# Moving the re-layout of a mode tensor from its load to its store: four mixing layers in one launch

## The chip, the cores and the metric

The program runs on one NeuronCore of a Trainium2 chip, in one launch. The metric is the time on the device in microseconds (us), from start to end of the program. The median of three runs of the kernel before is 8131.88 us (8118.62 to 8132.38).

## The reference, cut to what matters

The input is `x`, 16 images of 224 x 224 pixels with 32 channels, float32. Four layers follow each other, each of the form `x = x + layer(groupnorm(x))`. Only the last one is touched by the change:

```python
def _L3_conv_ref(x, R_real, R_imag):
    R = R_real + 1j * R_imag                       # (32, 32, 64, 64)
    kX, kY = R.shape[-2:]
    xt = jnp.moveaxis(x, -1, -3)
    xd = jsp_fft.dct(xt, type=2, axis=-1, norm='ortho')
    xf = jnp.fft.rfft(xd, axis=-2, norm='ortho')
    xtr = xf[..., :kX, :kY]                        # 64 x 64 modes are kept
    y = jnp.einsum('ijab,ejab->eiab', R, xtr)      # mix the channels, per mode
    yp = jnp.pad(y, ((0, 0), (0, 0), (0, nXf - kX), (0, nY - kY)))
    yr = jnp.fft.irfft(yp, n=nX, axis=-2, norm='ortho')
    yd = jsp_fft.idct(yr, type=2, axis=-1, norm='ortho')
    return jnp.moveaxis(yd, -3, -1)
...
x = x + _L3_conv_ref(_gn(x), L3_conv_R_real, L3_conv_R_imag)
```

So: for each of 16 images, 64 x 64 modes of 32 channels, each a complex number, are mixed over the channels by a matrix of their own, and are then taken back to pixels.

## The kernel before, in words

`program` (L1627) runs six passes one after the other, with nothing of one overlapping the next: `pass_fractal` (names a_), `mix_modes` for layer 1 (b1_), `pass_spectral` (c_), `pass_conv` (d_, which also makes the modes of layer 3 in `spec3`), `mix_modes` for layer 3 (b3_; the trace prints both calls as b_), and `pass_inverse` (e_). The last two are the ones touched.

**Mixing, third layer** (`mix_modes` with `groups=2`). The 64 x 64 modes of an image are folded into 2048 pairs: pair m = a' x 64 + b holds the modes (a', b) and (a' + 32, b), the fold being the index h of 0 and 1. The pairs are walked in 16 blocks of SC = 128. For a block SyncE (SP) loads 4 MB of matrices (`Rb`, L708, 32 KB per partition) and 1 MB of modes (`Xb`, L710, runs of 512 B) on its own DMA queue (q1). Both have two buffers, `par` 0 and 1. VectorE (DVE) negates a part of `Rb` (L744), scales `Xb` into the block diagonal `XB` (L746), both in two halves, and corrects one column (L750). TensorE (PE) makes 256 small matmuls (L783) into four PSUM banks. ScalarE (ACT) copies two of the banks into `Yb` (L799) and DVE the other two (L757). ACT then issues the stores to `y3` (L806) on its own DMA queue (q10): for each of 4 slot groups j and 2 folds h one DMA of 16 partitions (the 16 images) by 8 KB, 32 pairs of 64 floats, in one run on both sides. The next load into a buffer is issued when PE has done with it (`sp.wait_ge(mixed, ...)`). A `Yb` buffer is used again when its stores have landed: the waits on `out_[par]` stand before L757 on DVE and before L799 on ACT, each counting 16 x 8 = 128 for a block. PE waits for `low` and `high`, the two copies out of PSUM, of the block two before.

The 64 floats v of a pair are k x 32 + (re or im, channel half), where k is the half of the channels (even or odd channels).

**Inverse** (`pass_inverse`). For each of the 16 images SP loads, on q1, four mode pieces (L1448, one for each fold h and channel half k) and eight pieces of the residual `x3` (L1442, 784 KB each, runs of 1792 B) that is added at the end. A mode piece goes to 64 partitions (b) by 32 (a') by 32 floats:

```python
sp.dma_start(UT[64 * k:64 * k + 64, par, :, h, :],
             d["y3"][e, h].rearrange("(a b) v -> b a v", b=64)[:, :, 32 * k:32 * k + 32])
```

In `y3` and in `UT` the runs of this copy are 32 floats, 128 B. `UT` has two buffers, `X3` one, in four groups of 8 channels (lg). The modes and the residual of image e + 1 are issued as the groups of image e come free (`f_done`), the modes first. For each of 16 channel pairs cp, PE makes four matmuls over the columns (L1477: modes as weights, `UT`, two products of 224 columns, each in two passes), ACT copies the result to `V` (L1513), PE makes two products over the rows with the table `G3` (L1486; one row of the trace for each pass), and DVE adds the residual into `OUT` (L1532, four instructions). When 16 channel pairs are done GpSimd (POOL) issues eight stores of 784 KB to `out` (L1549) on its queue q0. PE runs at most two channel pairs ahead of DVE (`after(pe, sem["f_done"], e16 + (cp - 1))`).

`tables` (L1555) makes the constants on the host, among them `G3`, whose rows are in the order of the 128 rows of `V`: (a', fold h, re or im).

Of the kernel before, what the change touches and what calls it, by code (L numbers as in the profile page):

```python
# [27 lines left out]
C = 32  # L28
G = 16
T = 2  # L30
P = 128
# [46 lines left out]
def after(engine, sem, count):  # L78

    if not isinstance(count, int) or count > 0:  # L80
        engine.wait_ge(sem, count)  # L81
# [599 lines left out]
def mix_modes(nc, name, B, pairs, d, spec, out, R, acol, bcol, groups=1):  # L681
# [9 lines left out]
    nb = min(spec.shape[-1], SC)  # L691
    parts = SC // nb
    with Scope(nc, name) as z:
        Rb = z.sb("R", [P, 2, SC, 64])
# [35 lines left out]
        def _(dve):  # L730
# [22 lines left out]
            def collect(i, par):  # L753

                after(dve, out_[par], i * 128)
                dve.wait_ge(mixed, i * 4 + (2 * par + 2))
                dve.tensor_copy(Yb[:, par, SLOTS // 2:].rearrange("p s v -> p (s v)"),  # L757
                                PS[:, 4 * par + 2:4 * par + 4, :].rearrange("p k v -> p (k v)")).then_inc(high, 1)
# [34 lines left out]
        @block.scalar  # L793
        def _(act):
            def turn(i):
                for par in range(2):
                    after(act, out_[par], i * 128)
                    act.wait_ge(mixed, i * 4 + (2 * par + 1))
                    act.activation(Yb[:, par, 0:SLOTS // 2].rearrange("p s v -> p (s v)"),  # L799
                                   PS[:, 4 * par:4 * par + 2, :].rearrange("p k v -> p (k v)"), ACT.Copy)\  # L800
                       .then_inc(low, 1)
                    act.wait_ge(low, i * 2 + (par + 1))
                    act.wait_ge(high, i * 2 + (par + 1))
                    for j in range(4):
                        for h in range(2):
                            act.dma_start(out[:, h, bass.ds((i * 2 + par) * SC + SLOTS * j, SLOTS), :],  # L806
                                          Yb[32 * j + 16 * h:32 * j + 16 * h + B, par]).then_inc(out_[par], 16)

            turn(0)
            with act.Fori(1, n // 2) as i:  # L810
                turn(i)
            for par in range(2):
                act.wait_ge(out_[par], (n // 2) * 128)

# [602 lines left out]
def pass_inverse(nc, B, d, keep):  # L1417
# [5 lines left out]
    with Scope(nc, "e_") as z:  # L1423
        X3 = z.sb("X3", [R, NLG, T, NP, LG, NY])
        OUT = z.sb("OUT", [R, 2, T, W, C])
        UT = z.sb("UT", [P, 2, 32, 2, 32])
        V = z.sb("V", [P, 4, 2, W])
# [11 lines left out]
        def _(sp):  # L1439
# [5 lines left out]
            def load_modes(e, par):  # L1445
                for h in range(2):
                    for k in range(2):
                        sp.dma_start(UT[64 * k:64 * k + 64, par, :, h, :],  # L1448
                                     d["y3"][e, h].rearrange("(a b) v -> b a v", b=64)[:, :, 32 * k:32 * k + 32])\
                          .then_inc(ys_in[par], 16)  # L1450

# [20 lines left out]
        def _(pe):  # L1472
            def over_columns(e16, par, cp):
                after(pe, sem["vev_done"], e16 + (cp - 1))
                for k in range(2):
                    half = slice(64 * k, 64 * k + 64)
                    last = pe.matmul(PS[:, 2 * (cp % 2) + k, 0:W],  # L1477
                                     UT[half, par].rearrange("b a h (q c) -> b (a h q) c", c=C // 2)[:, :, cp],
                                     Di[half, :], start=True, stop=True)
                last.then_inc(sem["vps_ready"], 1)  # L1480
# [74 lines left out]
def tables():  # L1555
# [11 lines left out]
    for name, n in (("1", 32), ("3", 64)):  # L1567
# [16 lines left out]
        inv = np.stack([w * np.cos(ang), -w * np.sin(ang) * (a != 0)[:, None, None]], 1)  # L1584
        t["G" + name] = inv.reshape(2 * n, T, -1)

    bd = np.zeros((NYQ, YQ, CG, CG, 32))
# [100 lines left out]
```

## Time and profile before

| | us |
|---|---|
| median of three runs | 8131.88 |
| the profiled execution, its own time | 8130.66 |
| the span of its trace | 8129.0 |
| third mixing, first load to last store issued (7090.8 to 7413.4) | 323 |
| inverse, first load to the end (7416.2 to 8129.0) | 713 |

The granted TensorE clock of the profiled execution is 0.903 on average. A time such as 7203.11 is the place in the span. In the queue rows of the trace, q1 is SP's queue, q10 ACT's, q0 POOL's; "packets" are the single runs that the 16 DMA engines of the core move, and the share of a queue is the time of its packets over the time of 16 engines (packets of one engine overlap, so shares can add up to a little over 100%).

### The profile page before, as it was taken

Reading aid. Unit: us, or ns where it says so; the run is one execution under the profiler, and the core shown is the slowest. Engines: PE = TensorE matmul, PEld = TensorE weight load, DVE = VectorE, ACT = ScalarE, POOL = GpSimd, SP = SyncE. Lnnn points to the kernel's source line nnn. Section 1 sums busy time; section 2 is a strip of 40 time slices with the busy share of each in tenths; the row PEclk is TensorE's granted clock in tenths of the full one; section 3 lists DMA queues with packets and bytes.
Section 4 is the critical chain, followed back from the end, with each engine's and each line's share of the span. In section 5 each row is a group of like instructions: output and inputs, shape, how many; then the busy total and the mean of one; then the engine's idle time right before and its main releaser. Section 6 shows DMA issues by size and latency. Waiting matters only on the chain. (4 is left out here: it accounts for less than half of the span.)

```text
span 8129.0 us, 106295 instructions
## 1 busy us (share of the span) xinstructions
PE 6783.0 (83%) x35680; PEld 4281.1 (53%) x35680; DVE 5619.8 (69%) x10505; ACT 3651.6 (45%) x4902; POOL 321.2 (4%) x242
## 2 busy tenths in 40 slices
PE   5888888888888888668888888999999999636998
PEld 2455444445444545456666664666666565533443
DVE  8998999899999999645555565555555555266665
ACT  4776766676677666512222222343434334201111
POOL 0000000000000000000000000000000000000001
PEclk9998988898899888878898898999999999767999
DMA  1111111111111111364555548676666667399999
GB/s 78 70 70 70 70 70 70 70 70 69 70 70 69 61 58 54 115 191 152 183 160 162 175 160 211 161 181 165 173 173 168 174 164 180 104 317 279 318 332 304
DMA packets 796744, 1176.65 MB, mean 145 GB/s; under 512 B 216690, under 2 KB 698466, under 8 KB 779714
## 3 DMA queue, kind: packets, MB, share of 16 engines
q1 hardware_dynamic: 645058, 921.00, 37.7%
q10 hardware_dynamic: 133120, 140.54, 6.6%
q0 software_dynamic: 18176, 110.11, 3.3%
q8 instruction: 220, 3.60, 0.2%
q14 instruction: 170, 1.39, 0.1%
HBM read 706.59 MB, written 464.91 MB: 144 GB/s over the span
## 5 line engine op out<-in xcount | busy, mean ns | idle before, releaser
L432 PE MATMUL a_PS<-a_H,a_band 128*128 128x448 f32 x5120 | 2230.5, 594 | 396.3 <-DVE a_H L537 317.0
L432 PEld LDWEIGHTS a_PS<-a_H,a_band 128*128 128x128 f32 x5120 | 1046.3, 210 | 1421.8 <-issue 1214.2
L1221 PE MATMUL d_PS<-d_N,d_Bd 128*128 128x504 f32 x3072 | 1374.4, 599 | 85.2 <-ACT d_R L1328 60.1
L361 ACT ACTIVATE a_L<-a_PS,a_eps 128x896 f32<-128x896 f32 x1024 | 1025.1, 1001 | 597.2 <-PE a_PS L432 595.8
L1221 PEld LDWEIGHTS d_PS<-d_N,d_Bd 128*128 128x128 f32 x3072 | 576.8, 193 | 739.3 <-issue 734.4
L1404 DVE TENSOR_TENSOR d_X<-d_R,d_X 128x504 f32<-128x504 f32 x512 | 347.8, 679 | 879.6 <-ACT d_R L1328 876.5
L370 ACT ACTIVATE a_X<-a_L,a_alp 128x224 f32<-128x224 f32 x1024 | 816.2, 797 | 7.4 <-DVE a_L L546 7.4
L1079 DVE SCALAR_TENSOR_TENSOR c_XO<-c_PS,c_XC 128x128 f32<-128x128 f32 x1792 | 471.1, 407 | 363.2 <-PE c_PS L951 362.5
L1328 ACT ACTIVATE d_R<-d_PS,d_b 128x504 f32<-128x504 f32 x512 | 347.3, 681 | 783.2 <-PE d_PS L1221 671.2
L544 DVE TENSOR_TENSOR a_L<-a_L 128x1792 f32<-128x1792 f32 x256 | 517.4, 2021 | 243.3 <-ACT a_L L361 241.7
L1532 DVE TENSOR_TENSOR e_OUT<-e_PS,e_X 112x224 f32<-112x224 f32 x1024 | 429.9, 538 | 266.3 <-PE e_PS L1486 157.2
L350 ACT ACTIVATE a_H<-a_X,a_cf 128x448 f32<-128x448 f32 x512 | 380.4, 798 | 359.6 <-DVE a_H L537 294.3
L1231 PEld LDWEIGHTS d_PS<-d_F,d_XP 112*112 112x112 f32 x4096 | 486.4, 184 | 96.8 <-issue 57.7
L951 PEld LDWEIGHTS c_PS<-c_Ws,c_XT 128*128 128x128 f32 x3584 | 430.3, 197 | 189.0 <-ACT c_XT L1002 153.2
L1231 PE MATMUL d_PS<-d_F,d_XP 112*112 112x128 f32 x4096 | 491.6, 280 | 37.5 <-ACT d_XP L1288 37.5
L1486 PE MATMUL e_PS<-e_V,e_G 128*112 128x448 f32 x1024 | 461.5, 577 | 43.9 <-DVE e_OUT L1532 43.2
L1361 DVE TENSOR_SCALAR d_N<-d_X,d_cf 128x56 f32<-128x56 f32 (+1 forms) x1536 | 482.1, 372 | 17.0 <-DMA d_X<-tmp_x 9.6
L443 PEld LDWEIGHTS a_PS<-a_F,a_X 128*112 128x112 f32 x4096 | 457.9, 187 | 51.2 <-issue 48.2
L951 PE MATMUL c_PS<-c_Ws,c_XT 128*128 128x128 f32 x3584 | 472.9, 286 | 0.0
L443 PE MATMUL a_PS<-a_F,a_X 128*112 128x64 f32 x4096 | 464.8, 271 | 2.4 <-DVE a_X L552 2.4
L574 DVE TENSOR_TENSOR a_run<-a_run,a_X 128x896 f32<-128x896 f32 x448 | 466.0, 1081 | 0.0
L1002 ACT ACTIVATE c_XT<-c_PS 128x512 f32<-128x512 f32 x448 | 246.2, 595 | 414.5 <-PE c_PS L937 411.1
(183 smaller groups left out, 7447.3 us busy)
## 6 DMA issues: line engine op xcount, KB each, us to landing
d_X<-tmp_x SPq DMA_DIRECT2D x512, 252.0 KB, 5.0
a_X<-in_x SPq DMA_DIRECT2D x32, 3584.0 KB, 19.1
c_XC<-tmp_x SPq DMA_DIRECT2D x224, 512.0 KB, 3.9
tmp_x<-d_X SPq DMA_DIRECT2D x512, 204.8 KB
tmp_x<-a_X SPq DMA_DIRECT2D x32, 3136.0 KB, 18.3
tmp_x<-c_XO SPq DMA_DIRECT2D x32, 3136.0 KB, 19.3
d_XR<-tmp_x ACTq DMA_DIRECT2D x256, 392.0 KB, 5.6
e_X<-tmp_x SPq DMA_DIRECT2D x128, 784.0 KB, 16.7
```

What stands on the lines that cost most here:

```text
L361: act.activation(out, PS[:, b0:b0 + 2, 0:2 * W], ACT.Ln, bias=eps[:, 0:1]).then_inc(sem["ln_done"], 1)
L370: last = act.activation(X1[:, u % 4, :, k], L[:, u % 2, 0, :, k], ACT.Identity, scale=alp[:, 0, c:c + 1], bias=alp[:, 1, c:c + 1])
L432: last = pe.matmul(PS[:, 2 * (j % 2) + k, 0:2 * W], band[:, pos, :], Hb[:, u % 2, level, y1:y1 + HALF, :].rearrange("p y c -> p (y c)"), s ...
L443: last = pe.matmul(PS[0:YQ * CG, 4 + cg % 2, yq * 64:yq * 64 + 64], X1[:, (2 * cg + t) % 4, yq * YQ:yq * YQ + YQ, :].rearrange("p y c -> p ...
L544: steps.done(dve.tensor_tensor(lu[:, 0:2], lu[:, 0:2], lu[:, 2:4], ALU.subtract))
L574: steps.done(dve.tensor_tensor(run[:, j], first if k == 1 else run[:, j], now, op))
L951: last = pe.matmul(PS[:, bank + h, j * P:j * P + P], XT[:, n % 2, h, j * P:j * P + P], Ws[:, par], start=False, stop=(j == 3))
L1079: last = dve.scalar_tensor_tensor(out=XO[:, par, t, ph, :, 4 * q:4 * q + 4].rearrange("p c y -> p y c"), in0=PS[:, 2 + 2 * (n % 2) + h, :] ...
L1221: last = pe.matmul(PS[:, c % 2, 0:NW], Bd[:, c * 3 + s, :], N2[:, c % 4, :, s:s + NY], start=(s == 0), stop=(s == 2))
L1231: last = pe.matmul(PS[0:HALF, 2 + 2 * (cg % 2) + yc, k * P:k * P + P], XP[:, cg % 2, k, t, 2 * yc:2 * yc + 2, :].rearrange("p k y -> p (k ...
L1361: last = dve.tensor_scalar(N2[:, c % 4, b0:b1, 1:1 + NY], X2[:, cg % 4, b0:b1, k, :], cf[:, v, 0, c:c + 1], cf[:, v, 1, c:c + 1], ALU.mult ...
L1486: last = pe.matmul(PS[0:R, 4 + 2 * (cp % 2) + t, 0:2 * W], Gr[:, t, :], V[:, cp % 4].rearrange("p k y -> p (k y)"), start=True, stop=True)
```

## The change

The tensor `y3` gets the shape (image, channel half k, fold h, b 64, a' 32, 32 floats) instead of (image, fold h, pair 2048, 64 floats). The third mixing stores into it with sixteen DMAs per block instead of eight, each for one half of the channels, in runs of 32 floats; the inverse reads a mode piece with one run of 32 x 32 floats, 4 KB, per partition. The buffer `UT` and the rows of `G3` swap the order of fold h and a' to match. The first mixing (`groups=1`) keeps its stores.

```diff
@@ mix_modes
+    STORED = 128 * groups
...
-                after(dve, out_[par], i * 128)
+                after(dve, out_[par], i * STORED)
...
-                    after(act, out_[par], i * 128)
+                    after(act, out_[par], i * STORED)
...
                     for j in range(4):
                         for h in range(2):
-                            act.dma_start(out[:, h, bass.ds((i * 2 + par) * SC + SLOTS * j, SLOTS), :],
-                                          Yb[32 * j + 16 * h:32 * j + 16 * h + B, par]).then_inc(out_[par], 16)
+                            mine = Yb[32 * j + 16 * h:32 * j + 16 * h + B, par]
+                            if groups == 1:
+                                act.dma_start(out[:, h, bass.ds((i * 2 + par) * SC + SLOTS * j, SLOTS), :], mine)\
+                                   .then_inc(out_[par], 16)
+                                continue
+                            for k in range(2):
+                                act.dma_start(out[:, k, h, SLOTS * (j % 2):SLOTS * (j % 2) + SLOTS,
+                                                  bass.ds((i * 2 + par) * 2 + j // 2, 1), :].squeeze(2),
+                                              mine[:, :, 32 * k:32 * k + 32]).then_inc(out_[par], 16)
...
-                act.wait_ge(out_[par], (n // 2) * 128)
+                act.wait_ge(out_[par], (n // 2) * STORED)
@@ pass_inverse
-        UT = z.sb("UT", [P, 2, 32, 2, 32])
+        UT = z.sb("UT", [P, 2, 2, 32, 32])
...
-                        sp.dma_start(UT[64 * k:64 * k + 64, par, :, h, :],
-                                     d["y3"][e, h].rearrange("(a b) v -> b a v", b=64)[:, :, 32 * k:32 * k + 32])\
-                          .then_inc(ys_in[par], 16)
+                        sp.dma_start(UT[64 * k:64 * k + 64, par, h], d["y3"][e, k, h]).then_inc(ys_in[par], 16)
...
-                                     UT[half, par].rearrange("b a h (q c) -> b (a h q) c", c=C // 2)[:, :, cp],
+                                     UT[half, par].rearrange("b h a (q c) -> b (h a q) c", c=C // 2)[:, :, cp],
@@ tables
+        if name == "3":
+            t["G3"] = inv.reshape(hn, 2, 2, T, -1).transpose(1, 0, 2, 3, 4).reshape(2 * n, T, -1)
@@ kernel
-("y3", (B, 2, 2048, 64))
+("y3", (B, 2, 2, 64, 32, 32))
```

The order of the instructions moves at one place, ACT's stream in the loop of the third mixing. Before, from the last three stores of one block to the copy of the next (the ISA and REGISTER_ALU rows set up addresses and waits):

```order
L806 DMA tmp_y<-b_Y 16x2048
L806 ISA
L806 DMA tmp_y<-b_Y 16x2048
L806 ISA
L806 DMA tmp_y<-b_Y 16x2048
L798 REGISTER_ALU
L799 ACTIVATE b_Y<-b_PS 128x1024
L802 REGISTER_ALU
```

Eight such DMAs stand between two copies. With the change, the same place:

```order
L813 DMA tmp_y<-b_Y 16x32x32
L813 ISA
L813 DMA tmp_y<-b_Y 16x32x32
L813 ISA
L813 DMA tmp_y<-b_Y 16x32x32
L799 REGISTER_ALU
L800 ACTIVATE b_Y<-b_PS 128x1024
L803 REGISTER_ALU
```

Sixteen DMAs stand between two copies, each of half the bytes: 16 partitions by 32 runs of 32 floats in place of one run of 2048.

On SP's stream at the start of the inverse nothing changes places; only the form of the mode loads is another. Before, and with the change:

```order
L1461 DMA e_Di<-in_Di 128x224
L1461 DMA e_G<-in_G 128x224
L1448 DMA e_UT<-tmp_y 64x32x32 x4
L1442 DMA e_X<-tmp_x 112x4x448 x8
L1465 UNCONDITIONAL_BRANCH
```

```order
L1467 DMA e_Di<-in_Di 128x224
L1467 DMA e_G<-in_G 128x224
L1456 DMA e_UT<-tmp_y 64x1024 x4
L1450 DMA e_X<-tmp_x 112x4x448 x8
L1471 UNCONDITIONAL_BRANCH
```

A load of 64x32x32 is 2048 runs of 128 B, one of 64x1024 is 64 runs of 4 KB. The four mode loads of an image stand ahead of its eight residual loads as before.

## Rows read from the trace of the kernel before

**Rows 1.** The page: busy time by engine, DMA share in 40 slices.
```profile
PE 6783.0 (83%) x35680; PEld 4281.1 (53%) x35680; DVE 5619.8 (69%) x10505; ACT 3651.6 (45%) x4902; POOL 321.2 (4%) x242
DMA  1111111111111111364555548676666667399999
```
**Rows 2.** Stretches: mixing, first two images of the inverse, two later ones.
```profile
core 0: us, PE busy (x) PEld busy (x) DVE busy (x) ACT busy (x) POOL busy (x), PEclk, DMA share, GB/s
7091.00:7416.00 325.00, 95.67 (x4096) 92.78 (x4096) 217.49 (x98) 16.39 (x16) 6.74 (x1) 0.63 0.89 310
7425.00:7503.00 78.00, 77.00 (x253) 36.70 (x254) 51.22 (x122) 17.33 (x32) 4.26 (x8) 0.96 1.05 285
7579.00:7665.00 86.00, 79.16 (x257) 37.62 (x258) 53.85 (x130) 17.23 (x32) 8.32 (x16) 0.96 1.05 322
```
**Rows 3.** Timeline of the mixing, PE, SP, DVE: start, us, engine, line, what.
```profile
7196.50 6.38 PE L783 MATMUL b_PS<-b_R,b_XB 128*32 128x64 f32 x256 [14.85 <-DVE b_XB L750]
7234.65 6.09 PE L783 MATMUL b_PS<-b_R,b_XB 128*32 128x64 f32 x256 [18.13 <-DVE b_XB L750]
...
7203.11 0.33 SPq L708 DMA_DIRECT2D b_R<-in_R  x1
7240.97 0.33 SPq L708 DMA_DIRECT2D b_R<-in_R  x1
...
7222.29 2.28 DVE L744 TENSOR_SCALAR b_R<-b_R 32x4096 f32<-32x4096 f32 x1 [10.95 <-DMA b_X<-tmp_spec]
```
**Rows 4.** Timeline of the mixing: ACT issues the stores of a block.
```profile
7197.67 4.33 ACTq L806 DMA_DIRECT2D tmp_y<-b_Y  x8
7211.57 4.84 ACTq L806 DMA_DIRECT2D tmp_y<-b_Y  x8
7409.08 4.29 ACTq L806 DMA_DIRECT2D tmp_y<-b_Y  x8
```
**Rows 5.** Queues, 7211 to 7213, 7223 to 7229, 7231 to 7233: packets, MB, share.
```profile
q1 hardware_dynamic: 29, 0.95, 114.1%
q1 hardware_dynamic: 80, 2.62, 101.2%
q1 hardware_dynamic: 1156, 0.59, 110.9%
```
**Rows 6.** Queues, 7422 to 7424 (mode loads), 364 to 365 (stores of 512 B).
```profile
q1 hardware_dynamic: 3276, 0.42, 132.2%
q1 hardware_dynamic: 364, 0.18, 80.4%
```
**Rows 7.** DMA issues by line: duration in ns, min/median/max.
```profile
L1279 ACTq DMA_DIRECT2D d_XR<-tmp_x x256: 569/596/1427, 5005.9 to 7029.3; - x128
L1448 SPq DMA_DIRECT2D e_UT<-tmp_y x64: 632/1248/17762, 7417.1 to 8053.8; - x64
```
**Rows 8.** Inverse, queues: all in 7580 to 7588; 7634 to 7638; q0, q1 in 7602 to 7620.
```profile
DMA packets 8448, 1.36 MB, mean 171 GB/s; under 512 B 8272, under 2 KB 8448, under 8 KB 8448
...
q1 hardware_dynamic: 604, 1.05, 107.2%
...
q0 software_dynamic: 939, 5.93, 78.6%
q1 hardware_dynamic: 939, 1.63, 23.4%
```
**Rows 9.** Inverse, waits over 7416 to 8129: us in total, times, longest.
```profile
DVE e_OUT L1532 <- DMA e_X<-tmp_x: 109.1, 24, 22.8
```
**Rows 10.** Inverse, timeline of PE, and the last product in the chain that ended last.
```profile
7424.85 2.87 PE L1477 MATMUL e_PS<-e_Di,e_UT 64*128 64x224 f32 x12 [17.36 <-DMA e_UT<-tmp_y]
7603.27 1.76 PE L1486 MATMUL e_PS<-e_V,e_G 128*112 128x448 f32 x4
7605.67 1.76 PE L1486 MATMUL e_PS<-e_V,e_G 128*112 128x448 f32 x4
...
8101.69 1.74 PE e_PS L1486 x4
```

More of the change, by code:

```diff
@@ L1681 @@
     for name, shape in (("x1", (B, H, W, C)), ("x2", (B, ROWS2, NP, C, NY)), ("x3", (B, ROWS3, NP, C, NY)),
-                        ("spec1", (B, 16, P, 32)), ("y1", (B, 2, 512, 64)), ("spec3", (B, P, 2048)), ("y3", (B, 2, 2048, 64))):
+                        ("spec1", (B, 16, P, 32)), ("y1", (B, 2, 512, 64)), ("spec3", (B, P, 2048)), ("y3", (B, 2, 2, 64, 32, 32))):
         d[name] = nc.dram_tensor("tmp_" + name, shape, F32).ap()
```

## The prediction

> **What bounds the kernel now.** I read the page first. Over the whole span TensorE leads with 83% and the DMA engines are idle for the most part, but in the last six of the 40 slices, about 1000 us, the DMA share stands at nine tenths or more after one slice of three [rows 1]. That is where the change lies, so I split that end by stretches. In the third mixing PE is busy 96 of 325 us, DVE 217, and the DMA share is 0.89 at 310 GB/s; in two images of the inverse PE is busy 79 of 86 us and the DMA share is 1.05 at 322 GB/s [rows 2]. Both stages have full DMA engines, and in the inverse PE is close behind.
>
> *Mixing.* The timeline shows blocks in twos: PE starts buffer 0 at 7196.50 and again at 7234.65, 38.15 us later, and before each start it waits for DVE, which waits for the load [rows 3]. Buffer 0 is loaded from 7203.11, DVE takes it up at 7222.29, the load for its next use is issued at 7240.97: the loop is load, DVE, PE, load, and a longer load lengthens it one for one. Eight such periods make the stage.
>
> *Inverse.* The waits say that DVE stood 109 us for the residual [rows 9], and PE, at most two channel pairs ahead, stands behind DVE. Undisturbed, a channel pair takes 7605.67 - 7603.27 = 2.40 us, 38.5 us an image and 616 us for 16. The first product starts at 7424.85, the last ends at 8103.4 [rows 10]: 678.6 us, so 62 us is all that faster loads can give back within this stretch. The rest is the start and the last stores.
>
> **What the change removes.** 64 mode loads of 2048 packets of 128 B become 64 of 64 packets of 4 KB. In 8 us at 7580, 8272 small packets and 0.31 MB of residual moved [rows 8]. The residual alone runs at 1.05 MB in 4 us, 263 GB/s [rows 8], so it took 1.2 of them and the modes of an image take 6.8 us of full engines. As 4 KB packets the same 1.05 MB takes 4.0 us at the residual's 263 GB/s, or 2.4 us at the 2.62 MB in 6 us, 437 GB/s, of the 32 KB packets [rows 5]. Between 2.8 and 4.4 us an image goes. The first two images already run at PE's pace, busy 77 of 78 us [rows 2]; the other 14 took (678.6 - 77) / 14 = 43.0 us each, and for them that is 39 to 62 us. I take 42, near the lower end, since a stage whose DMA time (43.0 - 3.6 = 39.4 us an image) comes within a microsecond of PE's 38.5 keeps some waits. The very first mode load, for which PE waited 17.4 us together with the barrier [rows 10], gets about 3 us shorter. **Sum for the inverse: -45 us, bounds -20 (half of the freed time is lost to the residual, whose groups are freed one by one) and -65.** PE's products, their weights and DVE's and ACT's work are the same in number and shape; the order of the rows in `UT` and `G3` costs nothing, since PE reads weights at one fixed step of 16 floats in either layout. SP issues the four mode loads ahead of the residual: today it is held in one of them for up to 17.8 us [rows 7], because the queue is full. With 64 packets each they pass quickly, and what is late next is still the residual.
>
> **What it adds.** 131072 packets of 128 B now go out of `Yb`, to addresses 4 KB apart, in place of 128 DMAs of 16 x 8 KB. Two prices.
>
> *Issue.* A store DMA costs ACT 4.33 / 8 = 0.54 us today [rows 4]. For one with 512 runs the nearest row is the load of 448 runs, 596 ns in the median [rows 7]. Sixteen of them are 9.2 us a block in place of 4.3 to 4.8 [rows 4]; with the copy, ACT is held 20 of 38 us. Behind the issues on ACT stands only the copy of the next block (L799); PE needs it 38 us later for the same banks, DVE's copy doesn't wait for it. So inside the stage the issue is hidden. At the end it isn't: two blocks' issues follow each other, the last now begins at 7409.08 and would begin about 3 us later and last 4.9 us longer: **+8 us**, bounds +5 and +15.
>
> *DMA time.* Packets of R are 32 KB (29 of them in 0.95 MB) and take over 1 us each on an engine; though ACT issued stores from 7211.57, not one store packet stands between 7211 and 7213 [rows 4, 5]. Where two queues have work the engines take them in turn, packet for packet, as the inverse shows: 939 packets of q0 and 939 of q1 in the same 18 us [rows 8]. A store packet of 128 B gets one turn for each packet of the load: next to none beside R, some 128 of an engine's 512 beside the X load, the rest when no load is under way. So I add up DMA time. A period of two blocks has R at 2 x 4.19 MB / 437 GB/s = 19.2 us and X at 2 x 1.05 MB / 295 GB/s = 7.1 us [rows 5], which leaves 38.15 - 26.3 = 11.8 us for 1024 store packets on each engine: **11.5 ns a packet is the price at which the stage just keeps its pace.** Every ns above costs 1024 x 8 = 8.2 us in all.
>
> No row shows a store of 128 B. Below, the loads of 128 B: 3276 in 2 us over 16 engines, 9.8 ns each [rows 6]; by it the stage has 1.8 us of slack a period and loses nothing, and may gain up to 12 us, as the 8 KB store packets that now share turns with X, and lengthen a load, become short. Above, the stores of 512 B: 364 in 1 us over 16 engines, 44 ns [rows 6], if a packet costs the same whatever it holds: +33 ns, +266 us. By bytes that row gives 11 ns. I take 12.5 ns, nearest the row of the same size and just above the row of stores scaled by bytes, and that is **+8 us**, bounds -12 and +266.
>
> The Trainium skill, on its page "DMA: Bandwidth & Descriptors" (Specifications), says that below 512 B a DMA does a read-modify-write and doesn't reach line rate. By that rule the new stores are the wrong side to have the short runs on. On the side of loads the trace agrees in part, 209 GB/s for 128 B against 263 and 437; on stores it is silent.
>
> Waits: DVE's copy (L757) waits for the stores of its buffer from the period before, now counted to 256, and the two halves of the next `prepare` stand behind it. It is reached a period, 38 us, after those stores were issued, and ACT's issue ends within 5 us today [rows 4], so it bites only where the stores of a block take over 30 us, that is in the second rival.
>
> **The sum:** -45 + 8 + 8 = -29 on the profiled execution's 8130.7 (1.2 below the median of the runs): **8102 us.** A measurement of this kernel can tell about 0.2%, 16 us, from no change.
>
> **The rivals.**
> 1. *The two sides cancel.* A store packet costs 14 to 18 ns, 2.5 to 6.5 over the price of balance, +20 to +53 in the mixing, +8 at its end, -45 in the inverse: 8114 to 8147. For it: stores of 512 B are slower than X's loads of the same size (44 against 1156 in 2 us, 28 ns [rows 5, 6]). Against: those stores may be held by their issue, as the share of 80% there suggests.
> 2. *Short stores cost by the packet* (slower). At 25 ns the mixing needs 26.3 + 25.6 = 52 us for a period instead of 38: +110; at 44 ns it is +266. Less 37 for the rest: 8204 to 8360, from 18 ns on. DVE would then stand for `out_`, and PE behind it. For it is the 512 B row as it stands and the 4 KB step between writes, against it the loads of 128 B, also 16 KB apart in the tensor, that run at 9.8 ns. The page's rule above would make this the outcome; it gives no figure for it, twice the 9.8 ns would be +66 in the mixing and about 8160.
> 3. *The inverse drops fully to PE's pace and the mixing gains:* -60 and -5: 8066.
>
> **How the numbers follow.** Forecast (8078 to 8114) 0.42; rival 1: 0.21; rival 2 with its lower part from 8147: 0.31; rival 3: 0.06. Rival 1's band lies in the window of no change (8114 to 8147) for nearly all of it, some of its weight falls on either edge. Faster by over 0.2%: 0.48; within: 0.18; slower: 0.34. The range from 8074 to 8235 leaves out about 5 in 100 below and 13 above; the forecast's own is 8078 to 8114.
>
> **What would show it.** In the inverse: `e_UT` packets gone, period of two images from 86 to about 79 us, DVE's wait for `e_X` from 109 us to under 50, SP never over a few us in a mode load. In the mixing: period near 39 us; store packets bunched between the loads; ACT's sixteen issues at 9 to 10 us or stretched to 20 where the queue is full; the stage from 323 to some 340 us. I am wrong in the price of a short store if the period is over 43 us, wrong in the inverse if it stays above 82 us for two images, and wrong about the issue if one costs over 0.8 us where nothing is queued.

## The result, and the profile after

The change is slower: 8202.43 us in the median of four runs (8182.62 to 8240.06), against 8125.25 (8115.05 to 8132.38) for the kernel before on the same chip. The ratio is 1.0094, with a 95% interval of 1.0075 to 1.0114. The profiled execution is the slowest of the four: its own time is 8240.06 and its span 8238.4, and 37 us of that lie in passes that the change doesn't touch (the third mixing starts at 7127.7 in place of 7090.8), which is more than the median shows. The stages are therefore compared by their own length, the mixing from its first load to the first mode load of the inverse, and the inverse from there to the end:

| us | before | change |
|---|---|---|
| third mixing | 326.3 | 370.4 |
| inverse | 711.9 | 740.3 |

Both stages are longer, by 44 and by 28 us. Together that is 72, close to the 77 between the medians. Of the mixing's 44, 33 lie in its blocks and 11 at its end. Its last product starts 310.1 us after its first load before, 343.6 us with the change; and from that product to the first load of the inverse (issued at 7416.20 and 7497.29) it takes 15.3 us before and 26.0 with the change:

```profile
7400.93 6.55 PE L783 MATMUL b_PS<-b_R,b_XB 128*32 128x64 f32 x256 [6.84 <-DVE b_XB L750]
...
7471.31 5.25 PE L784 MATMUL b_PS<-b_R,b_XB 128*32 128x64 f32 x256 [9.23 <-DVE b_XB L751]
```

The page and the stretches of the change, which answer to [rows 1, 2]:

```profile
PE 6810.3 (83%) x35680; PEld 4295.0 (52%) x35680; DVE 5617.7 (68%) x10505; ACT 3649.5 (44%) x4902; POOL 320.8 (4%) x242
...
DMA  1111111111111110455445457666676665599999
```
```profile
core 0: us, PE busy (x) PEld busy (x) DVE busy (x) ACT busy (x) POOL busy (x), PEclk, DMA share, GB/s
7128.00:7496.00 368.00, 95.40 (x4096) 92.26 (x4096) 217.06 (x98) 16.37 (x16) 6.64 (x1) 0.61 0.91 274
7504.00:7582.00 78.00, 75.95 (x250) 36.41 (x251) 49.63 (x117) 17.30 (x32) 4.24 (x8) 0.95 1.03 299
7658.00:7744.00 86.00, 79.07 (x255) 36.95 (x253) 50.25 (x120) 16.65 (x31) 8.29 (x16) 0.94 1.05 305
```

The engines' work is the same. In the mixing the DMA share is as high as before with 274 GB/s in place of 310; in the later images of the inverse it is the same 1.05 with 305 in place of 322 GB/s, though all its short packets are gone.

**Mixing.** The timeline of PE, of ACT and of DVE, and the waits of the stage (us in total, times, longest), to be held against [rows 3, 4]:

```profile
7231.54 5.65 PE L784 MATMUL b_PS<-b_R,b_XB 128*32 128x64 f32 x256 [13.07 <-ACT b_Y L800]
7256.34 5.22 PE L784 MATMUL b_PS<-b_R,b_XB 128*32 128x64 f32 x256 [19.16 <-ACT b_Y L800]
...
7432.94 5.64 PE L784 MATMUL b_PS<-b_R,b_XB 128*32 128x64 f32 x256 [14.92 <-issue]
```
```profile
7230.46 1.02 ACT L800 ACTIVATE b_Y<-b_PS 128x1024 f32<-128x1024 f32 x1 [32.91 <-issue]
7231.66 23.44 ACTq L813 DMA_DIRECT2D tmp_y<-b_Y  x16
7255.22 1.02 ACT L800 ACTIVATE b_Y<-b_PS 128x1024 f32<-128x1024 f32 x1 [23.73 <-issue]
...
7486.38 8.61 ACTq L813 DMA_DIRECT2D tmp_y<-b_Y  x16
```
```profile
PE b_PS L784 <- ACT b_Y L800: 122.3, 7, 19.2
...
DVE b_Y L758 <- DMA tmp_y<-b_Y: 93.2, 11, 10.4
```

Before, PE waited for DVE, which waited for a load. Now PE waits for ACT's copy out of PSUM, and the copy waits for ACT itself, which spends 23.4 us in issuing the sixteen stores of the block before. Nine blocks lie between 7231.54 and 7432.94, 22.4 us each, against 19.1 before. In the first twelve blocks the sixteen issues take 18.2 to 32.6 us. In the last four, where no load of the mixing is left, they take 8.6 us, 0.54 us each. What holds them stands in the queues, at 7255 to 7256, 7258 to 7260, 7270 to 7272 and 7276 to 7278 (q1 the loads, q10 the stores; packets, MB, share):

```profile
q10 hardware_dynamic: 1460, 0.18, 116.9%
...
q10 hardware_dynamic: 1959, 0.24, 71.2%
...
q1 hardware_dynamic: 25, 0.82, 94.8%
q10 hardware_dynamic: 24, 0.00, 1.0%
...
q1 hardware_dynamic: 975, 0.50, 82.3%
q10 hardware_dynamic: 975, 0.12, 39.2%
```

Right behind a load, 1460 short packets go out in 1 us and the engines are full. A little later 1959 go out in 2 us, at 0.712 x 2000 x 16 / 1959 = 11.6 ns of an engine each, and the engines are busy for 71% only. That is the pace of ACT's issue: 512 packets in 0.54 us are 1900 in 2 us. Beside packets of `R`, 24 go out in 2 us: one for each packet of 32 KB. Beside packets of `X` it is one for one again, 975 to 975. So a block's 8192 short packets hardly move while `R` is loading, and where nothing is loading they move no faster than ACT issues them. The next load doesn't fill that time either: SP issues it at 7261.78, after PE's product of 7256.34, and PE had waited for ACT.

**Inverse.** The waits, and SP's issues of a mode load (duration in ns, min/median/max), against [rows 7, 9]:

```profile
DVE e_OUT L1538 <- DMA e_X<-tmp_x: 115.9, 25, 8.4
...
PE e_PS L1483 <- DMA e_UT<-tmp_y: 28.8, 1, 28.8
```
```profile
L1456 SPq DMA_DIRECT2D e_UT<-tmp_y x64: 468/816/10254, 7498.1 to 8152.9; - x64
```

PE's 28.8 us stood at 17.4 before [rows 10]. They begin in the mixing and hold its longer end: from the inverse's first load to its first product it takes 8.1 us (7505.41 - 7497.29), against 8.7 before, so the first mode load isn't slower. DVE waits for the residual as long as before, 116 against 109 us. The queues say why. First the whole inverse of the kernel before and 8 us in which it loads residual alone (7632 to 7640), then the same of the change (whole; 7512 to 7520; 7668 to 7676):

```profile
q1 hardware_dynamic: 191776, 119.78, 67.4%
q0 software_dynamic: 16384, 102.77, 35.1%
...
q1 hardware_dynamic: 1304, 2.25, 106.3%
```
```profile
q1 hardware_dynamic: 64800, 119.78, 66.6%
q0 software_dynamic: 16384, 102.77, 34.8%
...
q1 hardware_dynamic: 1379, 2.39, 106.9%
...
q1 hardware_dynamic: 1056, 1.83, 106.8%
```

A queue's share times the length is the time that its packets took: q1 took 0.674 x 712 = 480 us before and 0.666 x 740 = 493 after, with the same bytes and a third of the packets. So the residual's packets, untouched, must have become dearer by more than the mode loads became cheaper. The short rows show it: a residual packet took 1.063 x 8000 x 16 / 1304 = 104 ns before, 99 ns early in the change's inverse, and 129 ns later on. The packets of the whole inverse, sorted by size, give the sum (mean time of one, and all of them over 16 engines):

| | before | change |
|---|---|---|
| mode loads | 13.5 ns, 111 us | 271 ns, 69 us |
| residual | 102 ns, 366 us | 117 ns, 420 us |
| stores to `out` | 278 ns, 249 us | 286 ns, 256 us |

The mode loads gave back 42 us of full engines, the residual took 54 and the stores 7.

### The profile page after: what moved, and what is told of

Same layout as the page of the kernel before. It is cut to its first block and busy times, and to the rows that moved or that the text cites. A ratio compares the mean times of both kernels' runs of the same rounds, so it can differ in the third digit from the quotient of the medians.

```text
span 8238.4 us, 106647 instructions
## 1 busy us (share of the span) xinstructions
PE 6810.3 (83%) x35680; PEld 4295.0 (52%) x35680; DVE 5617.7 (68%) x10505; ACT 3649.5 (44%) x4902; POOL 320.8 (4%) x242
```

## The experiments

The ratio is to the kernel before on the same chip in the same batch, with its 95% interval; the stages are those of the profiled run, one execution each. The kernel before, profiled again, gave 325 and 718, the latter a little outside the 5 us expected. Five kernels with one and the same inverse (the change, e2, e4, e7, e11) gave 727 to 747 for it. So small differences in the inverse say nothing by themselves. The kernels e2, e4, e6, e8 and e13 to e16 don't compute the reference's result: they put the modes in another order, leave loads of them out, or take the residual from other places.

| run | what it is | ratio | mixing | inverse |
|---|---|---|---|---|
| (before) | | 1 | 326 | 712 |
| (change) | | 1.0094 [1.0075, 1.0114] | 370 | 740 |
| e1_short_stores | stores as changed, short loads on the inside of `UT` | 1.0061 [1.0044, 1.0078] | 368 | 713 |
| e2_long_loads | stores as before, loads as changed | 1.0019 [1.0009, 1.0030] | 327 | 747 |
| e4_sixteen_long | sixteen stores of 16 x 4 KB | one run | 322 | 734 |
| e5_long_both | pairs reordered, long on both sides | 1.0075 [1.0058, 1.0092] | 328 | 729 |
| e6_no_mode_loads | modes of images 2 to 15 not loaded | 0.9950 [0.9933, 0.9966] | 327 | 662 |
| e7_two_queues | the change, half the stores on POOL's queue | 1.0034 [1.0022, 1.0047] | 339 | 727 |
| e8_one_load | e2 with one load of 128 x 8 KB | 1.0025 [1.0013, 1.0037] | 327 | 742 |
| e9_long_both_one_load | e5 with one load | 1.0097 [1.0069, 1.0124] | 332 | 747 |
| e10_runs_512 | the change, loads in runs of 512 B | 1.0049 [1.0034, 1.0064] | 359 | 721 |
| e11_r_4k | the change, `R` in runs of 4 KB | 1.0069 [1.0044, 1.0094] | 365 | 731 |
| e12_both | e7, e10 and e11 together | 1.0025 [1.0013, 1.0037] | 341 | 719 |
| before_again | the kernel before | one run | 325 | 718 |
| e13_compact_src | e2, residual's source compact | 1.0009 [0.9994, 1.0023] | 327 | 737 |
| e14_res128_short | before, residual over 128 partitions | 0.9961 [0.9947, 0.9975] | 327 | 678 |
| e15_res128_long | e2, residual over 128 partitions | 0.9932 [0.9915, 0.9949] | 327 | 654 |
| e16_res128_one | e8, residual over 128 partitions | 0.9922 [0.9900, 0.9944] | 328 | 654 |
| e17_rows128 | before, row tiles of 128 rows | 1.0051 [1.0034, 1.0068] | 327 | 753 |
| e18_rows128_two_one | e17 with short stores on two queues, one load | 0.9972 [0.9957, 0.9986] | 336 | 673 |

### One half of the change at a time, and the DMA time taken away

e1 gives the inverse the order of `UT` of before, e2 writes `y3` as before (flat, eight stores), and reads it in runs of 4 KB. e5 orders the pairs b first, so that the copies of the mixing give long runs on both sides. e6 is the kernel before without its mode loads from image 2 on.

```diff
 # e1, against the change
-sp.dma_start(UT[64 * k:64 * k + 64, par, h], d["y3"][e, k, h])
+sp.dma_start(UT[64 * k:64 * k + 64, par, :, h, :], d["y3"][e, k, h])
 # e5, against the change
-Yb = z.sb("Y", [P, 2, SLOTS, 64])
+Yb = z.sb("Y", [P, 2, groups, SLOTS, 64 // groups])
-SO = z.sb("SO", [P, 2, 512])
+SO = z.sb("SO", [P, 64, 32])
 # e6, against the kernel before
-load_modes(e + 1, 1 - par)
...
+load_modes(1, 1)
```

> The stores are those of the change, the mode loads are in runs of 128 B as before (the buffer and its table as before, the output the reference's). Theory A: the whole loss is in the mixing, so this takes what the change takes, 8190 to 8215, and the mixing from first load to last store takes about 365 us as in the profile of the change. Theory B: the long loads do save 45 us in the change and the stores lose more than 77; this then takes about 8245.

> The stores are those of the kernel before (eight DMAs of 16 x 8 KB a block), the mode loads are those of the change (one run of 4 KB a partition). The modes then arrive in another order than the table expects, so the output is not the reference's. Theory A: in the trace of the change the first 4 KB mode packets moved at 226 to 266 GB/s, hardly above the 209 of the 128 B ones, so long loads give back little: no more than 10 us, 8115 to 8130. Theory B (the prediction's term for the inverse): 2.8 to 4.4 us an image, 8070 to 8090, and two images in 79 us.

> Long runs on both sides: the pairs are put in the order (b, a') from the convolution pass on, so that a block holds 4 b with all 32 a', and the copies out of PSUM put the two channel halves apart. Eight store DMAs of 16 partitions x 2 runs of 4 KB a block, mode loads of 4 KB runs, output the reference's. The modes are stored once an image (1 MB) and not in four pieces. Theory A: 8110 to 8130, no change against before. Theory B: 8070 to 8090.

> The kernel before with the mode loads of images 2 to 15 left out (the modes of the first two images are used again, so the output is not the reference's). It bounds from above what any form of these loads can give back. If the DMA engines bound the inverse and PE's pace is next, 14 images fall from 43.0 to at most 39 us: -50 to -62 us, 8065 to 8080. If the chain of single loads bounds it and not their sum, under 20 us come back.

The two halves are at fault on their own: the stores for the whole loss in the mixing (368), the loads for the loss in the inverse (747). The totals weren't expected, though: e1's 8178.98 us lies under both of its ranges, e2's 8158.11 over both of its.

e6 takes 50 us from the inverse, of the 62 that the prediction put as ceiling. Its wait for the residual, once at the start, and a stretch (columns as in the table of stretches above):

```profile
DVE e_OUT L1531 <- DMA e_X<-tmp_x: 28.4, 1, 28.4
...
7760.00:7840.00 80.00, 78.72 (x265) 37.73 (x265) 55.94 (x134) 17.82 (x34) 8.32 (x16) 1.00 1.04 322
```

So the loads did hold the stage before, as predicted, and with the mode loads gone PE's pace is left, 78.7 of 80 us. Both queues together took 661 us in place of 730. The mode loads left out were 98 us of it, and 29 went to the residual (108 ns a packet in place of 102) and the stores. Long loads free less, and lose more: in e2 the mode loads took 71 us in place of 111, and the residual 422 in place of 366.

e5 missed: its mixing keeps its pace (328), but the fourth pass, which writes the modes, became 37 us longer (2231 against 2194), and the inverse kept its loss.

### What holds the mixing

e4 keeps sixteen DMAs, each of 16 partitions by one run of 4 KB (a scrambled `y3`). e7 lets POOL issue the stores of k = 1 on its own queue. e11 lays `R` out so that its runs are 4 KB. e12 joins e7, e11 and e10 (below).

```diff
 # e4, against the change
-act.dma_start(out[:, k, h, SLOTS * (j % 2):..., bass.ds((i * 2 + par) * 2 + j // 2, 1), :].squeeze(2), mine[:, :, 32 * k:32 * k + 32])
+act.dma_start(flat[:, bass.ds(((i * 2 + par) * 8 + 2 * j + h) * 2 + k, 1), :].squeeze(1), mine.rearrange("e s v -> e (s v)")[:, SLOTS * 32 * k:SLOTS * 32 * k + SLOTS * 32])
 # e7, against the change
+pool.dma_start(out[:, 1, ...], Yb[32 * j + 16 * h:32 * j + 16 * h + B, par, :, 32:64]).then_inc(pout_[par], 16)
 # e11, against the change
-sp.dma_start(Rb[:, par], R[:, bass.ds(sc * SC, SC), :])
+sp.dma_start(Rb[:, par].rearrange("p (c m) v -> p c (m v)", m=16), R[bass.ds(sc * (SC // 16), SC // 16)].rearrange("c p n -> p c n"))
```

> The change with sixteen stores a block of 16 partitions x 4 KB in one run (the halves are not separated, so the modes are in another order and the output is not the reference's). It keeps the number of issues and the bytes, and takes the short packets away. If the number of issues holds the mixing: 350 us or more from its first load to the inverse's. If the number of packets does: 326 to 335. The inverse as with long loads, 740 to 747.

> The change, with the eight short stores of half k = 1 of each block issued from GpSimd's queue and the eight of k = 0 from ScalarE's, each with semaphores of its own; packets, bytes and addresses are the same. Theory Q (the mixing is held by one queue: one turn beside a 32 KB packet and 0.54 us an issue while no load runs): two queues take two turns and issue together, and the mixing falls from 368 us to 330 to 345; total about 8150 to 8170. Theory S (the price of a short store on the engines themselves): the mixing stays at 360 to 370, total 8190 to 8210.

> The change with the mixing matrices of the third mixing laid out so that they load in runs of 4 KB and not of 32 KB; stores, bytes and issues are the same, output the reference's. Theory Q: the short stores now get eight turns where they got one, 64 of a block's 512 packets on each engine beside R, and ScalarE is released sooner: the mixing falls from 370 to 345 to 358 us, total 8180 to 8195. If the turns don't matter (the price of a short store, or the issues) it stays at 365 to 372.

> The change with all three edits that spare the queues: short stores on two queues, R in runs of 4 KB, mode loads in packets of 512 B; output the reference's. If each does what its theory says: mixing 325 to 335, inverse 690 to 710, total 8110 to 8135, level with the kernel before or a little under it. If the length of the mode packets isn't the cause in the inverse: 8150 to 8170.

Sixteen issues cost nothing (322, in one run), so it is the number of packets behind them. Two queues give back 31 of the 44 us. Shorter packets of `R` give back 5: a miss. The turns were given, as 2 us of an `R` load in e11 show (7221 to 7223):

```profile
q1 hardware_dynamic: 193, 0.79, 95.9%
q10 hardware_dynamic: 194, 0.02, 7.9%
```

Eight times as many turns beside `R` aren't enough by themselves: they are 1024 of a block's 8192. e12 adds little to its parts, 341 in the mixing against e7's 339.

One rival of the number of packets is left. e10, below, changes nothing of the mixing but where the short runs land, 6 KB apart in place of 4 KB, and its mixing is 11 us shorter (359). Why is not shown.

e7 has two more causes that were not foreseen. Its queues over the whole mixing:

```profile
q1 hardware_dynamic: 35328, 83.89, 67.0%
q10 hardware_dynamic: 67584, 8.40, 16.2%
q0 software_dynamic: 4096, 8.40, 10.4%
```

For the same 8.4 MB ACT's queue shows 67584 packets and POOL's 4096. Take away the 2048 that end the 128 DMAs on 16 engines, and POOL's are 2048 packets of 4 KB, each a partition's 32 short runs. One turn would so move 32 runs, and the bytes take 0.104 / 0.162 of the time. Half of the short packets were gone, and ACT had eight issues a block in place of sixteen, as well as a second queue being there; these three are not told apart. All sixteen stores on POOL was not tried.

### What slows the residual

e8 has one mode load of 128 partitions by 8 KB, in place of four of 64 by 4 KB. e10 has runs of 512 B. e13 puts the residual's source in a compact order (its runs 2 KB apart) with e2's loads.

```diff
 # e8, against the change (stores as in e2)
-for h in range(2):
-    for k in range(2):
-        sp.dma_start(UT[64 * k:64 * k + 64, par, h], d["y3"][e, k, h]).then_inc(ys_in[par], 16)
+sp.dma_start(UT[:, par]..., d["y3"][e]....rearrange("(p n) -> p n", p=P)).then_inc(ys_in[par], 16)
 # e10, against the change
-("y3", (B, 2, 2, 64, 32, 32))
+("y3", (B, 2, 2, 64, 8, 192))      # 128 of each 192 floats are used
 # e13, against e2
-sp.dma_start(X3[:, lg, t], d["x3"][e, t * R:t * R + R, :, lg * LG:lg * LG + LG, :])
+off = (lg * 2 + t) * 204800
+sp.dma_start(X3[:, lg, t]..., d["x3"][e]...[off:off + R * NP * 512]....[:, :, 0:448])
```

> As e2_long_loads, but the modes of an image come in one DMA over all 128 partitions with 8 KB each, in place of four DMAs over 64 partitions with 4 KB each; again the modes are in another order than the table expects, so the output is not the reference's. Theory P (place): a DMA over 64 partitions makes engines wait for each other at the SBUF side or shifts them against one another, which is why 4 KB packets took 276 ns in the mean where the fastest took 159; over 128 partitions they take near 160 ns, the modes cost 3 us an image, and the inverse falls from 747 to 670 to 690 us, total 8085 to 8105. Theory L (length): a long packet ahead of the residual disturbs it wherever it goes; the inverse stays at 725 or more, total 8135 to 8165.

> The kernel e5_long_both with three edits, output the reference's: the modes of an image are loaded in one DMA of 128 partitions by 8 KB (the tensor y3 in the order image, half k, b, fold h, a', 32), the stores follow that order, and ScalarE's reordering copy in the convolution pass writes runs of 8 floats while it reads PSUM with a step, in place of writing with a step of 128 B (1043 ns against 597 before, 38 us over the pass). By theory P 8080 to 8105 if the copy is back at 600 ns, 8120 to 8145 if it isn't. By theory L 8145 or more.

> The change with a gap of 256 B after every 512 B of the mode tensor in memory, so that the same mode loads come in packets of 512 B (eight a partition in place of one of 4 KB), and nothing else; output the reference's. Theory L (length of the mode packets shifts the engines against each other and slows the residual, 1792 B packets of 118 ns in the mean with long mode packets against 102 with those of 128 B): with 512 B the residual is back near 102 to 106 ns and the modes themselves take under 5 us an image; the inverse falls from 740 to 690 to 710, total 8150 to 8175. If it isn't the length but that the modes pass quickly and the residual is issued early, the inverse stays at 730 or more, total 8190 to 8210.

> The kernel before, once more, for the spread of single stages between profiles: mixing 326 and inverse 712 within 5 us each by every theory; if the inverse lies above 725, the 740 of the change says nothing.

> e2_long_loads with the residual read from a compact piece of the tensor (rows of 1792 B at a step of 2 KB, 0.9 MB for a load) and not from rows 28 KB apart; the destination is as before, 112 partitions, 1792 B a packet (the output is not the reference's). Theory H: the mean of a residual packet falls from 118 to under 90 ns, inverse 650 to 690. Theory D: it stays at 110 to 125 ns, inverse 725 to 750.

Spreading a mode load over all partitions didn't help (742), and right behind the first such load the residual alone is slow. Queue of e8 at 7427 to 7435:

```profile
q1 hardware_dynamic: 967, 1.68, 107.4%
```

That is 142 ns a packet, against 99 in the change after four loads of 64 partitions; over the whole inverse the mean is 120, against 117. The place of the residual in memory isn't the cause (e13, 737, 116 ns in the mean). The length of the mode packets counts: in e10 the residual's mean falls to 108 ns, in e12 to 106. But runs of 512 B take 102 us themselves, where those of 4 KB take 69, and so the stage comes to 721 and 719, over the 690 to 710 expected. e9 repeated e5's longer fourth pass (2231), though ScalarE's copy there is as short as before; the one store an image that e5 and e9 share is left as its likely cause, untested.

### The residual over all 128 partitions

A residual load goes to 112 partitions, 16 x 7. e14 to e16 give the same number of bytes to 128 partitions, 16 x 8, in runs of 1568 B: on the kernel before, on e2, and on e8.

```diff
 # e14, against the kernel before
-X3 = z.sb("X3", [R, NLG, T, NP, LG, NY])
+X3 = z.sb("X3", [P, NLG, T, NP, LG, NY])
-sp.dma_start(X3[:, lg, t], d["x3"][e, t * R:t * R + R, :, lg * LG:lg * LG + LG, :])
+sp.dma_start(X3[:, lg, t]....[:, :, 0:392], d["x3"][e]....[t * 106:t * 106 + P, :, lg * 448:lg * 448 + 392])
```

> The kernel before with each residual load spread over 128 partitions (8 for each engine) in runs of 1568 B in place of 112 partitions (7 for each) in runs of 1792 B: the same bytes, 512 packets for 448. The rows 112 to 127 are not used and the tail of every run is zero, so the output is not the reference's. Theory D (the engines meet at the SBUF side, because of the split in sevens): the packets fall to 66 to 75 ns and the residual alone runs at over 330 GB/s, the inverse goes to PE's pace: 650 to 680 us, total 8075 to 8105. Theory H (they wait at the memory): 95 ns or more, inverse 705 to 725, total 8125 to 8145.

> e2_long_loads with the residual over 128 partitions as in e14_res128_short (output not the reference's, for both reasons). Theory D: as e14 or up to 15 us better, since nothing is left that the long packets disturb: 8065 to 8100. Theory H: as e2_long_loads, 8150 to 8165.

> e8_one_load (modes in one DMA of 128 partitions x 8 KB) with the residual over 128 partitions, so that every load of the inverse is split alike (output not the reference's). Theory D: the best of all, 8060 to 8090, mode packets near 309 ns. Theory H: as e8_one_load, 8150 to 8165.

Queues of e14 over the whole inverse, and at 7649 to 7657 (residual alone); then the inverse of e15:

```profile
q1 hardware_dynamic: 199968, 119.78, 59.1%
q0 software_dynamic: 16384, 102.77, 38.4%
...
q1 hardware_dynamic: 2040, 3.10, 105.3%
```
```profile
q1 hardware_dynamic: 72992, 119.78, 52.9%
q0 software_dynamic: 16384, 102.77, 40.2%
```

A residual packet takes 66 ns where it took 104, for 7/8 of the bytes, and the 8 us move 3.10 MB in place of 2.25; over the whole inverse the mean is 71 in place of 102. And now the change's loads pay: from e14 to e15 the time of q1 falls from 0.591 x 678 = 401 to 0.529 x 654 = 346 us, 55 less, where from the kernel before to e2 it rose by 16 (480 to 496). The stage goes from 678 to 654 only, since PE becomes the bound; a stretch of e15 (columns as in the table of stretches above):

```profile
7760.00:7840.00 80.00, 78.72 (x265) 37.71 (x264) 55.92 (x132) 17.78 (x33) 10.51 (x21) 1.00 0.97 354
```

PE is busy 78.7 of 80 us at a granted clock of 1.00.

### As whole kernels

In e17 each row tile takes 128 rows, 32 of them twice: rows 0 to 127 and 96 to 223. Runs stay at 1792 B. e18 adds the short stores on two queues and one mode load.

```diff
 # e17, against the kernel before
-X3 = z.sb("X3", [R, NLG, T, NP, LG, NY])
+X3 = z.sb("X3", [P, NLG, T, NP, LG, NY])
-sp.dma_start(X3[:, lg, t], d["x3"][e, t * R:t * R + R, :, ...])
+sp.dma_start(X3[:, lg, t], d["x3"][e, ROW0[t]:ROW0[t] + P, :, ...])
...
-OUT[:, par, t, y0:y0 + W // STORES, :]
+OUT[ONCE[t], par, t, y0:y0 + W // STORES, :]
 # e18, on e17
-("y3", (B, 2, 2048, 64))
+("y3", (B, 2, 64, 2, 32, 32))
+sp.dma_start(UT[:, par]..., d["y3"][e].rearrange("k b h a v -> (k b) (h a v)")).then_inc(ys_in[par], 16)
```

> The kernel before (long stores, 128 B mode loads), with one edit in the inverse: each of the two row tiles takes 128 rows (0 to 127 and 96 to 223, 32 of them twice) in place of 112, so the residual loads go to all 128 partitions, and the products over the rows and the residual addition with them; the stores take each row once. The runs of the residual stay 1792 B, and its bytes rise by 14% (512 packets a load in place of 448). The result is the reference's. Theory S (what slows the residual is that a load over 112 partitions gives each engine seven of them; over 128 the packets run at their own speed whatever their length): residual packets near 75 to 85 ns in place of 102, the inverse 675 to 700 in place of 712 to 718, the total 15 to 40 us under the kernel before, ratio 0.995 to 0.998. Theory B (the gain in the three runs with 128 partitions came from the shorter runs of 1568 B alone): packets stay at 100 ns or more, and with 14% more bytes the inverse is 725 to 750, the total 10 to 30 us over the kernel before.

> The inverse with row tiles of 128 rows as in the run before, and with it the change's idea in its cheapest form: the short stores of a block issued by two engines on two queues (ScalarE the even channels, GpSimd the odd ones), and one mode load of 128 partitions by 8 KB an image. The result is the reference's. Both theories expect the mixing at 337 to 342 (326 before), as with two queues alone. Theory S: the mode loads' time that is saved now stays saved, the inverse 655 to 675, the total 8085 to 8115, ratio 0.993 to 0.998, and no worse than the run with row tiles alone. Theory B: the residual packets are slowed by the long mode packets as in the change, 110 ns or more with 14% more bytes, the inverse over 735, the total 8170 or more.

Queues of e17: the whole inverse, and 7744 to 7752 (residual alone); then of e18: the whole inverse, and 7638 to 7646.

```profile
q1 hardware_dynamic: 199968, 134.48, 58.8%
q0 software_dynamic: 16384, 102.77, 37.3%
...
q1 hardware_dynamic: 1786, 3.11, 105.4%
```
```profile
q1 hardware_dynamic: 70176, 134.47, 54.6%
q0 software_dynamic: 16384, 102.77, 42.1%
...
q1 hardware_dynamic: 1749, 3.04, 104.8%
```

e17 missed on the time and settled the packets. A residual packet of 1792 B takes 1.054 x 8000 x 16 / 1786 = 76 ns, so the number of partitions does it, and not the run length: by bytes that is the speed of e14's packets, 42 ns for 1000 B in both, against 58 in the kernel before. Other numbers than 112 and 128 were not tried. But with 14% more bytes, and stores that take 0.373 x 753 = 281 us where they took 250, both queues together take 724 us against 730 before, so nothing was to be gained. Why the stage is then 41 us longer, the sum doesn't tell, and it stays open. A stretch of it shows PE a little less busy than before and the DMA engines not quite full:

```profile
7680.00:7760.00 80.00, 71.10 (x230) 34.86 (x228) 47.21 (x114) 15.11 (x29) 8.32 (x16) 0.95 0.97 316
```

e18 is where the parts meet. Its residual packets stay at 77 ns beside the long mode packets, q1 takes 0.546 x 673 = 367 us, 76 less than in e17, and the stage is 80 us shorter. After paying 10 us in the mixing, the kernel computes the reference's result in 8118.87 us against 8138.63: 0.28% faster than the kernel before (0.14 to 0.43%), 1.2% faster than the change by the two ratios, and 4 us over the range expected. It is the only whole kernel of the study that beats both.

## Why the prediction was wrong

The forecast was 8102 us, faster; it came out slower, at 8202, inside the range but on the other side. In the stages: -45 was forecast for the inverse and +28 measured, +16 for the mixing and +44 measured.

- *What bounds the two stages:* right. Both are full of DMA time, and e6 shows it for the inverse: without mode loads -50 us, and PE's pace is left, where the ceiling was put at 62.
- *"As 4 KB packets the same 1.05 MB takes 4.0 us ... or 2.4 us":* **the step that failed in the inverse**, in what it left unsaid: that the residual, 1.2 of the 8 us in which both moved, and all the time behind it, would keep its 263 GB/s. The term for the mode loads by themselves was near: 111 - 69 = 42 us of full engines were freed, 2.6 us an image, where 2.8 to 4.4 was said. But the residual's packets went from 102 to 117 ns in the mean, +54 us, and those of the stores cost 7 more. The change's 1.83 MB in 8 us is 229 GB/s. That is +20 us of queue time; the other 8 of the stage's 28 are not accounted for. The -45 us (bounds -20 and -65) had no bound above zero, though nothing in the trace excluded it.
- *"So inside the stage the issue is hidden":* **the step that failed in the mixing**. The price of an issue was right where the queue has room (8.6 us for sixteen, 9.2 forecast). That beside `R` a store packet gets one turn for each packet of the load was said one paragraph later, with its consequence only for the packets: that they'd fill the gaps. They fill ACT's queue first, ACT is held up to 32.6 us a block, and its next copy with it, for which PE stands 122 us. A period of two blocks went from 38.15 to 44.8 us. e7 and e4 confirm it from two sides.
- *The price of a short store, 12.5 ns of an engine:* right as the time of a packet, 11.6 ns alone and 0.392 x 2000 x 16 / 975 = 12.9 beside `X`. But the prediction counted its rows as packets over time, and so counted the stores alone went out at 2000 x 16 / 1959 = 16.3 ns, the pace of ACT's issue. The Trainium skill's rule on transfers below 512 B ("DMA: Bandwidth & Descriptors", Specifications) named the right side to fear, yet not by the price of a packet: the 19.6 ns that the prediction tried for it, twice its 9.8 ns for loads, doesn't show.
- *Adding up DMA time over a period* (26.3 + 1024 x price): 38 us by 11.6 ns, measured 44.8. The sum holds only if the stores can use every gap. At 7258 they use 71% of one. With 16.3 ns it gives 26.3 + 16.7 = 43.0 us. So the prediction's own sign, a period over 43 us, came true, and doesn't mean what it was to mean: the period was too long without a dear packet.
- *The wait of DVE's copy, to bite only "where the stores of a block take over 30 us":* it stood 93 us, since stores issued 23 us late also land late.
- *The rivals:* the second gave 8204 to 8360 from dear packets. The time came out just under its lower end, by luck and for another reason: cheap packets, few turns. The first rival gave the mixing +20 to +53 by a price of 14 to 18 ns; +33 before the stage's end lies inside, and the 16.3 ns too, again through ACT's issue and not the packet. The loss in the inverse, 28 of the 72 us, had no rival at all.
- *The end of the stage, +8:* about right, 26.0 - 15.3 = 10.7 us, within its bounds of +5 and +15. Not two but four blocks' issues follow each other there.
- *The very first mode load, 3 us shorter:* 0.5 us.

What is not shown: why packets to 112 partitions are dearer than packets to 128, why long mode packets in between make them dearer still, and why e10's mixing is shorter.

## What to carry to other kernels

Before a layout moves its short runs from one side of a tensor to the other, ask which engine issues them and what is queued behind that issue: thousands of short packets beside 32 KB ones leave at one for one, and the engine waits with them. Where a stage is bound by DMA time, don't add up packets at their old prices: the price of those not touched may move, here by 15% in the mean, and a look at the neighbour's packets in a one-edit run tells it sooner than any sum. Where a load goes to fewer than 128 partitions, try the same bytes over 128 early: here that took 34 us off the inverse, more than any change of run length did. It has to be the same bytes: with 14% more of them (e17) the stage was 41 us longer, for a reason that stays open.

## What was not expected of the hardware

- The same residual packets of 1792 B to 112 partitions took 99 ns early and 129 ns later in one and the same stage, 142 behind one long load, and 76 ns when loaded to 128 partitions.
- Stores of 128 B runs issued by POOL leave as packets of 4 KB; issued by ACT, as packets of 128 B.
- ScalarE's copy of 128 x 512 into steps of 128 B took 1042 ns, against 597 into a plain row (the fourth pass of e5, then of the kernel before):

```profile
L1313 ACT ACTIVATE d_SO<-d_PS 128x512 f32<-128x512 f32 x64 | 66.7, 1042 | 199.3 <-PE d_PS L1250 199.3
...
L1305 ACT ACTIVATE d_SO<-d_PS x64: 597/597/598, 5109.9 to 7087.6; 128x512 f32<-128x512 f32 x64
```
